# One attention and feed-forward layer on one Trainium2 core: softmax reciprocals spread over the partitions by DMA, heads normalised two pairs at a time, one more pair of heads in split products

## The chip, the cores and the metric

The kernel runs on one core of a Trainium2 chip. The metric is the device time of one execution in microseconds (us). The engines are PE (TensorE, matrix products), DVE (VectorE), ACT (ScalarE), POOL (GpSimd) and SP (SyncE, which issues the DMAs).

## The reference

The input is x of shape (16, 256, 128): 16 batches of 256 tokens. What is computed, cut to what matters:

```python
h = layernorm(x) * (1 + ca) + sa
q = h @ Wq                        # 16 heads of 64
k, v = split(h @ Wkv)             # 4 heads of 64 each, every one shared by 4 heads of q
q, k = rotary(q), rotary(k)
attn = softmax(q @ k.T * 64 ** -0.5)
x = x + ga * ((attn @ v) @ Wo + bo)
h = layernorm(x) * (1 + cb) + sb
x = x + gb * (gelu(h @ bin(w1).T + b1) @ bin(w2).T + b2)
```

`sa, ca, ga, sb, cb, gb` come from a small product with the input c, one row for each batch; `bin` keeps the signs of a weight and one scale for each output.

## The kernel before, in words

Every engine has a program written out by hand, and semaphores are the only order between engines. The attention runs over the 16 batches in steps (`attention_steps`); a step has 8 slots, and a slot works on one pair of heads. The table `SLOTS` is the order of the work inside a step: each string is a slot, each word a piece of work, and every engine walks through the same words and does its own part of each. The pieces overlap three batches: a step does the attention of its own batch, prepares q, k and v of the next one, and finishes the batch before.

The words: `S0` and `S1` are the two score products of a pair (PE), followed by the exponentials (ACT). `m` is a product with v of the pair before (PE, `product_with_v`): a pair in `SPLIT_PAIRS` is computed in six fp32r products of split operands, for which ACT computes the exponential twice (`probs`, `probs_hi`) and POOL subtracts (`probs_lo`); the other pairs take two plain fp32 products. `s0` to `s15` find the row maxima of a head (PE product, DVE reduction), `mT0` to `mT3` transpose them four heads at a time. `qkv..`, `kt`, `qt` make q and k; `yT` is the product with Wo, `zT` brings it back to the residual.

At the start of a slot ACT copies the unnormalised output of an older pair, with its row of softmax sums, from PSUM to `o_un` (word `un`, line 668). The eight pairs of a batch form half 0 (pairs 0 to 3) and half 1 (pairs 4 to 7). For each half SP gathers the sums into `sums` over 128 partitions (`gather_sums`, line 438), DVE takes the reciprocals and splits them in two fp32r parts (`recip0`, `recip1`, lines 790 to 794), SP writes those into `recip_parts` (`spread_reciprocals`, line 445), and for each pair a PE product with the constant `select` (words `bc0` to `bc7`, line 967) repeats them over 64 partitions for each head. DVE multiplies `o_un` by that, once for each head (line 777), into `o_t`, which `yT` reads.

SP has one queue and issues in program order, waiting on a semaphore ahead of each DMA. Besides the sums and reciprocals it moves, for each four heads of a batch, the high parts of q (`high_parts`, line 425: 64 partitions of 4 KB) and the transposed maxima (`maxima`, line 431, into partition 64 of `q_him`). The scores of slots 0, 2, 4 and 6 wait for both of these:

```python
if s % 2 == 0 and jc == 0:
    pe.wait_ge(q_him_in[s // 2], st.count(32, 32))
```

A last step (`tail`) finishes batch 15 beside the feed-forward part, which then runs over all batches.

Of the kernel before, what the change touches and what calls it, by code (L numbers as in the profile page):

```python
# [72 lines left out]
def parsed(slots):  # L73

    every, n, found = " ".join(slots).split(), 0, []
    for text in slots:
        slot, product = [("un",)], 0
        for word in text.split():
# [53 lines left out]
SPLIT_PAIRS = (1, 3, 4, 5, 7)  # L132
# [74 lines left out]
def slot_parts(st, s):  # L207

    if st.tail and s > 1:
        parts = [("part", u, part, part == PARTS[u[0]] - 1) for _, u in units(st, s) for part in range(PARTS[u[0]])]  # L210
        return [("recip", 1)] * (s == TAIL_RECIPROCALS_AT) + parts
    held = {"scores": st.attn, "pv": st.attn if s >= 1 else st.out, "un": st.attn if s >= 2 else st.out,
            "stats": st.norm, "rstd": st.norm, "norm": st.norm}
    return [w for w in ORDER[s]
            if (not st.tail and has(st, w[1]) if w[0] == "part" else not st.tail and (st.attn, st.out)[w[1]] if w[0] == "recip"
# [52 lines left out]
def adaln_layer(nc, x, wq, wkv, wo, bo, w1, b1, w2, b2, c, wmod, cos, sin, out):  # L268
    ctx = ExitStack()
    with ctx:  # L270
# [51 lines left out]
        q_him = [sb(f"q_him{i}", [DH + 1, 4, N], F32R) for i in range(2)]  # L322
# [4 lines left out]
        o_un = sb("o_un", [DH + 1, PAIRS, 2, N])  # L327
# [3 lines left out]
        recip_hi = sb("recip_hi", [P, 16], F32R)  # L331
        recip_lo = sb("recip_lo", [P, 16], F32R)
# [70 lines left out]
        def _(sp):  # L403
# [44 lines left out]
            def step(st):  # L448
# [6 lines left out]
                if st.out:  # L455
                    spread_reciprocals(st, 1, -1)
# [671 lines left out]
```

## Time and profile before

| | |
|---|---|
| median of 3 runs | 700.21 us (699.74 to 702.76) |
| the profiled execution | 700.25 us, span from first to last instruction 698.5 us |
| PE busy | 668.9 us (96%) |
| ACT, DVE, POOL busy | 551.4, 516.5, 430.1 us |
| mean granted TensorE clock | 0.99 |

How to read it: the span is what the trace covers, and the time of the execution is 1.75 us more. A busy share tells how long an engine had something under way, not that it ran at its peak. In the steady part one step, that is one batch, takes 37.7 us (the product with Wo comes back at that spacing).

### The profile page before, as it was taken

The numbers are of one execution on the slowest core, as the hardware profiler recorded it, in microseconds if no ns is written. First come the engines' busy times: TensorE is split into PE (matmuls) and PEld (weight loads), VectorE is DVE, ScalarE is ACT, GpSimd is POOL, SyncE is SP. The second block draws the span as 40 slices with busy tenths as digits, with TensorE's granted clock in tenths as the row PEclk, the third lists the DMA queues.
The fourth block names the chain that finished last, engine by engine and source line by source line (L and its number), as shares of the span: only waits on it lengthen the run. The fifth ranks groups of instructions, "written<-read, shape, count | busy, mean of one in ns | idle before, by whom it ended". The sixth has DMA issues, their size and how long they took to land.

```text
span 698.5 us, 13530 instructions
## 1 busy us (share of the span) xinstructions
PE 668.9 (96%) x3733; PEld 519.5 (74%) x3733; DVE 516.5 (74%) x1196; ACT 551.4 (79%) x1149; POOL 430.1 (62%) x397
## 2 busy tenths in 40 slices
PE   4698999999999999999999999999999999998897
PEld 3566787877777787878787777778787878667786
DVE  6566777778788777777787778887777877778762
ACT  4478887888787888878887878787887888768676
POOL 1657685857686776768585768577676758543110
PEclk9699999999999999999999999999999999999999
DMA  8111111011111111111102111111111110200111
GB/s 241 31 32 33 33 26 39 18 38 28 32 31 32 32 20 29 32 32 32 31 16 43 20 32 31 32 32 28 26 27 33 32 34 18 48 17 3 39 39 46
DMA packets 31580, 24.75 MB, mean 35 GB/s; under 512 B 16688, under 2 KB 26944, under 8 KB 31552
## 3 DMA queue, kind: packets, MB, share of 16 engines
q1 hardware_dynamic: 31552, 24.40, 16.6%
q8 instruction: 14, 0.23, 0.2%
q14 instruction: 14, 0.11, 0.1%
HBM read 4.47 MB, written 2.10 MB: 9 GB/s over the span
## 4 chain that ended last, share of the span: by engine, by line
PE 90%; DVE 3%; ACT 3%; POOL 1%; issue 1%; DMA 0%; SPq 0%; POOLq 0%; DVEq 0%
PE o_ps L1021 15%; PE o_ps L1011 11%; PE unit_ps L957 9%; PE score_ps L992 8%; PE unit_ps L946 8%; PE score_ps L994 8%; PE unit_ps L973 8%; PE o_ps L1078 4%; PE unit_ps L931 3%; PE unit_ps L932 3%; PE unit_ps L933 3%; PE unit_ps L967 2%; PE unit_ps L961 2%; PE unit_ps L1055 1%; PE unit_ps L1056 1%
## 5 line engine op out<-in xcount | busy, mean ns | idle before, releaser
L521 POOL TENSOR_TENSOR probs_lo<-probs,probs_hi 128x512 fp32r<-128x512 f32 x160 | 202.1, 1283 | 67.7 <-ACT probs_hi L662 67.6
L772 DVE TENSOR_REDUCE w_all<-unit_ps 128x2 f32<-128x512 f32 x256 | 166.2, 685 | 52.4 <-PE unit_ps L957 50.9
L659 ACT ACTIVATE probs<-score_ps 128x512 f32<-128x512 f32 x256 | 150.6, 589 | 21.2 <-PE score_ps L994 18.6
L507 POOL TENSOR_TENSOR rot_sum<-rot_a,rot_b 128x512 f32<-128x512 f32 (+1 forms) x96 | 104.7, 1097 | 99.3 <-DVE rot_b L764 99.0
L511 POOL TENSOR_TENSOR qk_rot<-rot_sum,qk_rot 128x512 fp32r<-128x512 f32 (+1 forms) x96 | 105.0, 1101 | 36.3 <-ACT qk_rot L609 36.3
L957 PEld LDWEIGHTS unit_ps<-k_hi,q_hilo 128*128 128x128 f32 x512 | 88.7, 191 | 41.3 <-issue 17.9
L957 PE MATMUL unit_ps<-k_hi,q_hilo 128*128 128x256 f32 x512 | 118.3, 318 | 0.7 <-ACT q_hilo L591 0.4
L946 PEld LDWEIGHTS unit_ps<-ident_r,qk_rot 128*128 128x128 f32 x640 | 101.9, 194 | 17.7 <-issue 4.3
L946 PE MATMUL unit_ps<-ident_r,qk_rot 128*128 128x128 f32 x640 | 110.2, 264 | 4.6 <-POOL qk_rot L511 3.8
L992 PE MATMUL score_ps<-q_hilo,k_hi 128*128 128x512 f32 x256 | 112.9, 441 | 1.1 <-DMA q_him<-neg_max_t 1.1
L777 DVE TENSOR_TENSOR o_t<-o_un,unit_ps 64x256 f32<-64x256 f32 x248 | 103.5, 417 | 4.4
L994 PE MATMUL score_ps<-q_him,k_lo 65*128 65x512 f32 x256 | 101.4, 396 | 0.0
L1011 PE MATMUL o_ps<-probs,v_whole 128*65 128x512 f32 x192 | 98.0, 592 | 0.0
L662 ACT ACTIVATE probs_hi<-score_ps 128x512 fp32r<-128x512 f32 x160 | 94.1, 588 | 0.0
L591 ACT ACTIVATE q_hilo<-unit_ps 128x512 fp32r<-128x512 f32 x128 | 76.4, 597 | 9.2 <-PE unit_ps L946 9.0
L668 ACT ACTIVATE o_un<-o_ps 65x512 f32<-65x512 f32 x128 | 74.4, 581 | 1.4 <-PE o_ps L1021 0.6
L762 DVE TENSOR_TENSOR rot_a<-unit_ps,cos_sb 128x512 f32<-128x512 f32 (+1 forms) x96 | 57.2, 596 | 21.6 <-PE unit_ps L961 17.1
L992 PEld LDWEIGHTS score_ps<-q_hilo,k_hi 128*128 128x128 f32 x256 | 48.5, 189 | 16.3 <-issue 8.9
L1021 PE MATMUL o_ps<-probs_hi,v_hi 128*65 128x512 f32 x160 | 60.3, 395 | 0.0
L1021 PE MATMUL o_ps<-probs_hi,v_lo 128*65 128x512 f32 x160 | 59.9, 411 | 0.0
L973 PE MATMUL unit_ps<-o_t,wo_sb 128*128 128x128 f32 x480 | 59.5, 277 | 0.0
L609 ACT ACTIVATE qk_rot<-rot_sum 128x512 fp32r<-128x512 f32 (+1 forms) x96 | 52.3, 561 | 6.7 <-POOL rot_sum L507 6.7
(120 smaller groups left out, 1123.4 us busy)
## 6 DMA issues: line engine op xcount, KB each, us to landing
q_him<-q_hilo SPq DMA_DIRECT2D x64, 256.0 KB
out_x<-w_all SPq DMA_DIRECT2D x16, 128.0 KB, 1.8
xa<-in_L_attn_x SPq DMA_DIRECT2D x3, 640.0 KB, 7.5
q_him<-neg_max_t SPq DMA_DIRECT2D x64, 4.0 KB
w_all<-in_L_attn_Wq SPq DMA_DIRECT2D x1, 512.0 KB, 5.3
w_sb<-in_L_ffn_w SPq DMA_DIRECT2D x2, 256.0 KB, 3.0
wo_sb<-in_L_attn_Wo SPq DMA_DIRECT2D x1, 512.0 KB, 8.2
sums<-o_un SPq DMA_DIRECT2D x32, 8.0 KB, 2.0
```

The costliest lines, as they stand in the source:

```text
L507: pool.tensor_tensor(total, rot_a[k % 2][:, 0:heads, :], rot_b[k % 2][:, 0:heads, :], ALU.add).then_inc(rot_summed, 1)
L511: pool.tensor_tensor(low, total, high.bitcast(F32), ALU.subtract).then_inc(rot_ready, 1)
L521: pool.tensor_tensor(probs_lo[s % 2][:, jc, :, :], probs[s % 2][:, jc, :, :], probs_hi[s % 2][:, jc, :, :].bitcast(F32), ALU.subtract).the ...
L659: ins = act.activation(probs[s % 2][:, jc, :, :].rearrange("p h i -> p (h i)"), score_ps[jc][:, :], ACT.Exp, scale=SCALE)
L772: dve.tensor_reduce(neg_max[u[1] // 4][:, first:first + C], ps[:, :].rearrange("p (c j) -> p c j", c=C), AX.X, ALU.max, negate=True).then_ ...
L946: ins = pe.matmul(ps[:, part * P:(part + 1) * P], qk_rot[:, ch, first + h, :, :].rearrange("p t d -> p (t d)"), ident_r[:, :], start=True, ...
L957: ins = pe.matmul(ps[:, ch * N:(ch + 1) * N], q_hilo[par][:, h, ch * P:(ch + 1) * P], k_hi2[par][:, g, :], start=True, stop=True)
L973: ins = pe.matmul(ps[:, own], wo_sb[:, s, :], o_t[:, s, own], start=s == 0, stop=s == PAIRS - 1)
L992: pe.matmul(ps[:, :], k_hi2[par][:, g, js], q_hilo[par][:, hs, :].rearrange("p h i -> p (h i)"), start=True, stop=False)
L994: pe.matmul(ps[:, :], k_lo1[par][:, g, js], q_him[s // 2 % 2][:, s % 2 * 2:s % 2 * 2 + 2, :].rearrange("p h i -> p (h i)"), start=False, s ...
L1011: ins = pe.matmul(o_ps[i][0:DH + 1, :], v_whole[par][:, jc, g, :], probs[i][:, jc, :, :].rearrange("p h i -> p (h i)"), start=jc == 0, sto ...
L1021: ins = pe.matmul(o_ps[i][0:DH + 1, :], v[par][:, jc, g, :], p[i][:, jc, :, :].rearrange("p h i -> p (h i)"), start=part == 0, stop=part == 5)
```

## The change

The reciprocals no longer pass through PE. After DVE has taken the 128x16 reciprocals of a half, one DMA writes them as one row of 2,048 values in a single partition (`reciprocals_to_row`, partition 96 for half 0 and 97 for half 1, in spare rows of the `q_him` buffer). When that has landed, two DMAs (`reciprocals_to_all`) copy the row's two parts of 1,024 values (4 KB) to 64 partitions each, into `o_t`. Another DMA (`second_heads`) moves the second heads of a half from partitions 0 to 63 of `o_un` to partitions 64 to 127. DVE then multiplies two pairs with both heads in one operation of 128x512 (`normalise_heads`, words `mul0` to `mul3`) in place. The `bc` words, `select`, `recip_parts` and the split of the reciprocals are gone. Pair 2 joins `SPLIT_PAIRS`. The table of slots is dealt anew: `mul0` and `mul1` stand in slot 0 of the next step, `mul2` and `mul3` at the end of slot 3. ACT's copy into `o_un` now waits for the multiplication that read the place before.

```diff
...
-    "S0 s9 m recip1 s10 qt6 qt6 qt6 qt6 m S1 s11 m m m m qkv00 mT2",
-    "qkv10 S0 m s12 m m S1 bc4 bc5 qt7 qt7 qt7 qt7 m bc6 m m s13",
-    "S0 bc7 S1 m s14 m s15 kt0 m kt0 stats kt0 rstd kt0 kt1 norm m m kt1 kt1 kt1 m mT3 yT0",
...
+    "S0 m recip1 s9 s10 m m S1 s11 qt6 m qt6 qkv00 qt6 m qt6 mT2 m",
+    "S0 s12 m m S1 qkv10 kt0 m m qt7 qt7 qt7 qt7 kt0 mul2 m kt0 s13 kt0 m mul3",
+    "S0 m s14 m s15 S1 kt1 m stats kt1 m rstd kt1 m kt1 m yT0 mT3",
...
+    "S0 qkv01 yT1 m m norm S1 qt0 m qt0 m qt0 qt0 m qt1 qt1 recip0 qt1 qt1 m qt2 qt2 zT0 zT0 qt2 qt2",
+    "S0 s0 m s1 s2 m m m s3 S1 m m qkv11 mT0",
...
+TAIL_PRODUCTS_AT = 6
+TAIL_AT = {("yT", 0): 7, ("yT", 1): 8, ("zT", 0): 9}
...
-SPLIT_PAIRS = (1, 3, 4, 5, 7)
+SPLIT_PAIRS = (1, 2, 3, 4, 5, 7)
...
-        q_him = [sb(f"q_him{i}", [DH + 1, 4, N], F32R) for i in range(2)]
+        q_him_all = sb("q_him_all", [P, 8, N], F32R)
+        q_him = [q_him_all[:, 4 * i:4 * i + 4, :] for i in range(2)]
+        recip_rows = [q_him_all[96 + i:97 + i, :, :].bitcast(F32) for i in range(2)]
         neg_max_t = [sb(f"neg_max_t{i}", [4 * C, P], F32R) for i in range(2)]
         probs = [sb(f"probs{i}", [P, C, 2, N]) for i in range(2)]
         probs_hi = [sb(f"probs_hi{i}", [P, C, 2, N], F32R) for i in range(2)]
         probs_lo = [sb(f"probs_lo{i}", [P, C, 2, N], F32R) for i in range(2)]
-        o_un = sb("o_un", [DH + 1, PAIRS, 2, N])
+        o_un = sb("o_un", [P, 2, 2, 4, N])
...
-        recip_hi = sb("recip_hi", [P, 16], F32R)
-        recip_lo = sb("recip_lo", [P, 16], F32R)
-        recip_parts = [sb(f"recip_parts{i}", [P, N], F32R) for i in range(2)]
-        select = sb("select", [P, PAIRS, DH], F32R)
...
-                    sp.dma_start(recip_parts[half][first:first + PAIRS, :].bitcast(F32).rearrange("h (b t) -> h b t", t=16),
-                                 part[:, :].bitcast(F32)).then_inc(recip_in[half], 16)
+                sp.dma_start(sums[:, :], o_un[DH:DH + 1, half, :, :, :]
+                             .rearrange("o h s (b t) -> o (h s b) t", t=16)).then_inc(sums_in[half], 16)
+
+            def second_heads(st, half, batch):
+
+
+                sp.wait_ge(sums_in[half], st.count(16, 16, batch))
+                sp.dma_start(o_un[DH:P, half, 0, :, :].rearrange("p s i -> p (s i)"),
+                             o_un[0:DH, half, 1, :, :].rearrange("p s i -> p (s i)")).then_inc(second_in[half], 16)
+
+            def reciprocals_to_row(st, half, batch):
+
+                sp.wait_ge(recip_ready, st.count(2, half + 1, batch))
+                sp.dma_start(recip_rows[half][:, :, :].rearrange("o h (b t) -> o (h b) t", t=16),
+                             recip[:, :]).then_inc(rows_in[half], 16)
+
+            def reciprocals_to_all(st, half, batch):
+
+
+                sp.wait_ge(rows_in[half], st.count(16, 16, batch))
+                if half == 0 and not st.prep:
+                    sp.wait_ge(z_ready, B - 1)
+                for h in range(2):
+                    sp.dma_start(o_t[h * DH:h * DH + DH, 4 * half:4 * half + 4, :].rearrange("p s i -> p (s i)"),
+                                 recip_rows[half][:, 4 * h:4 * h + 4, :].rearrange("o s i -> o (s i)").unsqueeze(1).broadcast_to([1, DH, 4 * N])).then_inc(recip_in[half], 16)
 
             def step(st):
                 if st.attn:
@@ -453,15 +469,21 @@
                 if st.attn:
                     high_parts(st, 2, 0)
                 if st.out:
-                    spread_reciprocals(st, 1, -1)
+                    second_heads(st, 1, -1)
+                    reciprocals_to_row(st, 1, -1)
+                    reciprocals_to_all(st, 1, -1)
                 if st.attn:
                     maxima(st, 2, 0)
                     high_parts(st, 3, 0)
                     maxima(st, 3, 0)
                     gather_sums(st, 0, 0)
-                    spread_reciprocals(st, 0, 0)
+                    second_heads(st, 0, 0)
+                    reciprocals_to_row(st, 0, 0)
                 if st.prep:
                     high_parts(st, 0, 1)
+                if st.attn:
+                    reciprocals_to_all(st, 0, 0)
+                if st.prep:
                     maxima(st, 0, 1)
...
+                            pair = (s - 2) % 8
+                            if st.number != 0 and pair < 4:
+                                act.wait_ge(o_t_ready, st.count(4, pair // 2 + 1, -1))
+                            act.activation(o_un[0:DH + 1, pair // 4, :, pair % 4, :],
+                                           o_ps[s % 2][0:DH + 1, :].rearrange("p (h i) -> p h i", h=2),
                                            ACT.Copy).then_inc(o_un_ready, 1)
...
-                if kind == "bc":
-
-                    for h in range(2):
-                        ins = dve.tensor_tensor(o_t[h * DH:h * DH + DH, u[1], :], o_un[0:DH, u[1], h, :],
-                                                ps[h * DH:h * DH + DH, 0:N], ALU.mult)
-                    ins.then_inc(o_t_ready, 1)
...
                 dve.wait_ge(sums_in[half], st.count(16, 16, batch))
                 dve.reciprocal(recip[:, :], sums[:, :]).then_inc(recip_ready, 1)
-                dve.wait_ge(recip_ready, st.count(2, half + 1, batch))
-                dve.tensor_copy(recip_hi[:, :], recip[:, :]).then_inc(recip_hi_ready, 1)
-                dve.wait_ge(recip_hi_ready, st.count(2, half + 1, batch))
-                dve.tensor_tensor(recip_lo[:, :], recip[:, :], recip_hi[:, :].bitcast(F32),
-                                  ALU.subtract).then_inc(recip_lo_ready, 1)
+
+            def normalise_heads(st, quarter, batch):
+
+                half, two = quarter // 2, slice(2 * quarter, 2 * quarter + 2)
+                own = slice(quarter % 2 * 2, quarter % 2 * 2 + 2)
+                if quarter % 2 == 0:
+                    dve.wait_ge(second_in[half], st.count(16, 16, batch))
+                    dve.wait_ge(recip_in[half], st.count(32, 32, batch))
+                dve.tensor_tensor(o_t[:, two, :], o_un[:, half, 0, own, :], o_t[:, two, :], ALU.mult).then_inc(o_t_ready, 1)
...
-                    half = u[1] // 4
-                    if u[1] % 4 == 0:
-                        pe.wait_ge(recip_in[half], st.count(32, 32, ahead(u)))
-                    ins = pe.matmul(ps[:, 0:N], select[:, 2 * (u[1] % 4):2 * (u[1] % 4) + 2, :].rearrange("k h d -> k (h d)"),
-                                    recip_parts[half][:, :], start=True, stop=True)
...
```

SP's program in the first step of the loop, from the gathering of the sums of half 1 to the maxima of heads 8 to 11 (`q_him` is called `q_him_all` after the change). Before:

```order
L438 DMA sums<-o_un 128x1x16 [waits o_un_ready]
L424 REGISTER_ALU
L425 DMA q_him<-q_hilo 64x1024 [waits q_ready]
L443 ISA
L445 DMA recip_parts<-recip_hi 8x16x16 [waits recip_lo_ready]
L445 DMA recip_parts<-recip_lo 8x16x16
L430 REGISTER_ALU
L431 DMA q_him<-neg_max_t 1x8x128 [waits max_t_ready]
```

After the change, the same place:

```order
L438 DMA sums<-o_un 128x1x16 [waits o_un_ready]
L424 REGISTER_ALU
L425 DMA q_him_all<-q_hilo 64x1024 [waits q_ready]
L444 ISA
L445 DMA o_un<-o_un 64x1024 [waits sums_in1]
L450 ISA
L451 DMA q_him_all<-recip 1x128x16 [waits recip_ready]
L461 DMA o_t<-q_him_all 64x1x1024 [waits rows_in1]
L461 DMA o_t<-q_him_all 64x1x1024
L430 REGISTER_ALU
L431 DMA q_him_all<-neg_max_t 1x8x128 [waits max_t_ready]
```

Two small DMAs have become four: one of 64 partitions, the row, and two copies from one partition to 64 each. The DMA of the maxima stands behind all of them, and SP waits for the row to land before it goes on. For half 0 the same four stand ahead of the maxima of heads 0 to 3 of the next batch, with one difference: the high parts of those heads are issued between the row and the two copies.

DVE's program in slot 3 of the same step. Before, two of the four pairs of half 1, then the row maxima of head 13:

```order
L777 TENSOR_TENSOR o_t<-o_un,unit_ps0 64x256 [waits unit_full]
L777 TENSOR_TENSOR o_t<-o_un,unit_ps0 64x256
L744 REGISTER_ALU
L777 TENSOR_TENSOR o_t<-o_un,unit_ps2 64x256 [waits unit_full]
L777 TENSOR_TENSOR o_t<-o_un,unit_ps2 64x256
L744 REGISTER_ALU
L772 TENSOR_REDUCE w_all<-unit_ps3 128x2 [waits unit_full]
```

After the change, from the rotation of q ahead of it to the same maxima:

```order
L783 TENSOR_TENSOR rot_a1<-unit_ps2,cos_sb 128x512 [waits rot_summed]
L785 TENSOR_TENSOR rot_b1<-unit_ps2,sin_sb 128x512
L814 TENSOR_TENSOR o_t<-o_un,o_t 128x512 [waits recip_in1,second_in1]
L765 REGISTER_ALU
L793 TENSOR_REDUCE w_all<-unit_ps0 128x2 [waits unit_full]
L814 TENSOR_TENSOR o_t<-o_un,o_t 128x512
```

Behind the multiplication that waits for the copies (`recip_in1`) stand the row maxima of head 13 and all that follows on DVE.

## Rows read from the trace of the kernel before

**Rows 1.** The page: span, busy time of each engine, share of the DMA queue.

```profile
span 698.5 us, 13530 instructions
PE 668.9 (96%) x3733; PEld 519.5 (74%) x3733; DVE 516.5 (74%) x1196; ACT 551.4 (79%) x1149; POOL 430.1 (62%) x397
q1 hardware_dynamic: 31552, 24.40, 16.6%
```

**Rows 2.** The page: the chain that ended last.

```profile
PE 90%; DVE 3%; ACT 3%; POOL 1%; issue 1%; DMA 0%; SPq 0%; POOLq 0%; DVEq 0%
```

**Rows 3.** Windows: one step; two start windows. Busy by engine, granted clock, DMA share, GB/s.

```profile
core 0: us, PE busy (x) PEld busy (x) DVE busy (x) ACT busy (x) POOL busy (x), PEclk, DMA share, GB/s
137.80:175.50 37.70, 37.68 (x214) 29.04 (x213) 29.09 (x63) 30.91 (x65) 26.11 (x24) 1.00 0.16 30
20.00:30.00 10.00, 6.91 (x26) 5.89 (x27) 3.50 (x10) 7.14 (x13) 6.74 (x8) 0.50 0.00 0
30.00:40.00 10.00, 8.39 (x44) 6.30 (x44) 6.28 (x11) 5.40 (x13) 3.71 (x3) 0.84 0.27 54
```

**Rows 4.** Who waited for whom: PE's scores on the DMA of the maxima.

```profile
PE score_ps L992 <- DMA q_him<-neg_max_t: 1.1, 2, 0.7
PEld score_ps L992 <- DMA q_him<-neg_max_t: 1.0, 1, 1.0
```

**Rows 5.** Groups by line and form: count, busy us, mean ns, idle before.

```profile
L967 PE MATMUL unit_ps<-recip_parts,select 128*128 128x256 f32 x124 | 49.0, 436 | 0.0
L1011 PE MATMUL o_ps<-probs,v_whole 128*65 128x512 f32 x192 | 98.0, 592 | 0.0
L521 POOL TENSOR_TENSOR probs_lo<-probs,probs_hi 128x512 fp32r<-128x512 f32 x160 | 202.1, 1283 | 67.7 <-ACT probs_hi L662 67.6
L662 ACT ACTIVATE probs_hi<-score_ps 128x512 fp32r<-128x512 f32 x160 | 94.1, 588 | 0.0
L777 DVE TENSOR_TENSOR o_t<-o_un,unit_ps 64x256 f32<-64x256 f32 x248 | 103.5, 417 | 4.4
L794 DVE TENSOR_TENSOR recip_lo<-recip,recip_hi 128x16 fp32r<-128x16 f32 x32 | 22.2, 694 | 1.1
L792 DVE CAST recip_hi<-recip 128x16 fp32r<-128x16 f32 x32 | 10.3, 321 | 1.1
```

**Rows 6.** The chain in order of time: start us, us, piece.

```profile
309.62 0.93 PE o_ps L1021 x4
314.06 0.24 PE unit_ps L967 x2
314.69 0.86 PE o_ps L1011 x2
```

**Rows 7.** Windows around single DMAs (columns as in rows 3).

```profile
5.50:7.00 1.50, 0.00 (x0) 0.00 (x0) 1.43 (x5) 0.63 (x1) 0.71 (x1) 1.00 0.93 303
292.77:294.24 1.47, 1.47 (x10) 1.05 (x8) 1.00 (x3) 0.04 (x1) 0.92 (x1) 1.00 0.87 176
291.41:291.59 0.18, 0.18 (x3) 0.18 (x3) 0.04 (x1) 0.18 (x1) 0.00 (x0) 1.00 0.50 46
287.17:287.67 0.50, 0.50 (x7) 0.50 (x6) 0.30 (x1) 0.45 (x1) 0.12 (x1) 1.00 0.15 17
286.57:286.67 0.10, 0.10 (x3) 0.10 (x3) 0.10 (x1) 0.10 (x2) 0.00 (x0) 1.00 0.22 41
```

**Rows 8.** Timeline of SP: when those DMAs were issued.

```profile
285.26 0.67 SPq L431 DMA_DIRECT2D q_him<-neg_max_t  x1
285.98 0.55 SPq L438 DMA_DIRECT2D sums<-o_un  x1
290.13 0.65 SPq L445 DMA_DIRECT2D recip_parts<-recip_hi  x1
291.59 0.53 SPq L425 DMA_DIRECT2D q_him<-q_hilo  x1
```

**Rows 9.** Issue to landing of the sums' DMA, min/median/max.

```profile
DMA to landing us min/median/max: 2.0/2.0/2.1
```

**Rows 10.** Timeline: the two reciprocals of a step, and the scores four heads ahead.

```profile
288.04 0.25 DVE L790 RECIPROCAL recip<-sums 128x16 f32<-128x16 f32 x1 [0.57 <-DMA sums<-o_un]
297.81 0.40 PE L992 MATMUL score_ps<-q_hilo,k_hi 128*128 128x512 f32 x1
308.78 0.24 DVE L790 RECIPROCAL recip<-sums 128x16 f32<-128x16 f32 x1
315.74 0.40 PE L992 MATMUL score_ps<-q_hilo,k_hi 128*128 128x512 f32 x1
```

More of the change, by code:

```diff
@@ L210, in slot_parts @@
         parts = [("part", u, part, part == PARTS[u[0]] - 1) for _, u in units(st, s) for part in range(PARTS[u[0]])]
-        return [("recip", 1)] * (s == TAIL_RECIPROCALS_AT) + parts
+        return ([("recip", 1)] * (s == TAIL_RECIPROCALS_AT)
+                + [("mul", 2), ("mul", 3)] * (s == TAIL_PRODUCTS_AT) + parts)
     held = {"scores": st.attn, "pv": st.attn if s >= 1 else st.out, "un": st.attn if s >= 2 else st.out,
-            "stats": st.norm, "rstd": st.norm, "norm": st.norm}
+            "stats": st.norm, "rstd": st.norm, "norm": st.norm, "recip": (st.attn, st.out), "mul": (st.out,) * 4}
     return [w for w in ORDER[s]
-            if (not st.tail and has(st, w[1]) if w[0] == "part" else not st.tail and (st.attn, st.out)[w[1]] if w[0] == "recip"
+            if (not st.tail and has(st, w[1]) if w[0] == "part" else held[w[0]][w[1]] and not (st.tail and s > 1 - w[1] // 2) if w[0] in ("recip", "mul")
                 else held[w[0]])]
@@ L437, in gather_sums @@
                 sp.wait_ge(o_un_ready, st.count(8, 4 * half + 4, batch))
-                sp.dma_start(sums[:, :], o_un[DH:DH + 1, 4 * half:4 * half + 4, :, :]
-                             .rearrange("o s h (b t) -> o (s h b) t", t=16)).then_inc(sums_in[half], 16)
-            def spread_reciprocals(st, half, batch):
-                sp.wait_ge(recip_lo_ready, st.count(2, half + 1, batch))
-                for first, part in ((0, recip_hi), (32, recip_lo)):
-                    sp.dma_start(recip_parts[half][first:first + PAIRS, :].bitcast(F32).rearrange("h (b t) -> h b t", t=16),
-                                 part[:, :].bitcast(F32)).then_inc(recip_in[half], 16)
+                sp.dma_start(sums[:, :], o_un[DH:DH + 1, half, :, :, :]
[15 more added lines that the diff above has]
+                                 recip_rows[half][:, 4 * h:4 * h + 4, :].rearrange("o s i -> o (s i)").unsqueeze(1).broadcast_to([1, DH, 4 * N])).then_inc(recip_in[half], 16)
             def step(st):
@@ L553, in _ @@
             act.activation(ident_r[:, :], ident[:, :], ACT.Copy).then_inc(ident_r_ready, 1)
-            for half in range(2):
-                act.activation(select[32 * half:32 * half + 32, :, :],
-                               ident[0:32, 0:PAIRS].unsqueeze(2).broadcast_to([32, PAIRS, DH]), ACT.Copy).then_inc(select_ready, 1)
             act.wait_ge(wkv_in, 16)
@@ L901, in wait_for_reader @@
                     pe.wait_ge(max_t_ready, st.count(4, u[1] + 1, of))
-                if kind == "bc":
-                    pe.wait_ge(o_t_ready, st.count(8, u[1] + 1, of))
                 if kind == "yT":
@@ L1044, in mlp_step @@
                     pe.wait_ge(max_t_ready, 4 * B)
-                    pe.wait_ge(o_t_ready, 8 * B - 4)
                     pe.wait_ge(x2_ready, B - 1)
```

34 lines of the change are left out of this document (15 added, 19 removed), and 8 rows, old and new, of the table SLOTS.

## The prediction, made before the changed kernel ran

> **What bounds the kernel now.** I read the page first. PE is busy for 96% of the span, the next engine, ACT, for 79% [rows 1], and 90% of the chain that ended last is PE's own work, with DMA at 0% [rows 2]. The window of one step in the steady part says the same: 37.68 us of PE work in 37.70 us, beside 29.0 on DVE, 30.9 on ACT and 26.1 on POOL [rows 3]. So PE sets the time, at the rate of one instruction behind another, and every other engine has 7 to 12 us to spare in a step. The DMA engines are 16% busy. The one place where a DMA could reach PE is the wait of the scores for the maxima: it cost 1.1 us in two places, and 1.0 in a third, in the whole run [rows 4]. That wait is covered now with little to spare, and it is what I look at in the change.
>
> The profiled execution took 700.25 us, its span 698.5; the median of the runs is 700.21, so the sum below can start from 700.2.
>
> **What the change takes off PE.** The chain gives start-to-start costs, which the mean durations (436 and 592 ns, overlapped [rows 5]) don't. Two `bc` products cost 0.24 us [rows 6], and there are 128 (124 of them in the group in [rows 5]): 128 x 0.12 = 15.4 us. Pair 2 was two plain products of 0.86 us each (the trace has two records for each), and becomes six split ones, four of which cost 0.93 us [rows 6]: 1.72 - 1.40 = 0.32 us, 16 times, 5.1 us. Together PE loses 20.5 us of work, 1.3 us a step.
>
> **What it adds elsewhere, and why that is hidden.** ACT gets two more exponentials a step (2 x 0.59 us [rows 5]): 30.9 + 1.2 = 32.1 us. POOL gets two more subtractions of 1.28 us: 26.1 + 2.6 = 28.7 us. Both stay under the 36.4 us that PE would then need. DVE loses 16 multiplications of 0.417 us and the split of the reciprocals, and gets four of 128x512. These are not in the trace; the nearest group is 0.417 us for half the columns, so 0.4 to 0.9 us each, 3.6 us at most for the 7 taken off. One thing may make them longer: `recip_lo`, on 16 columns with both operands in SBUF, takes 694 ns in the mean where the cast beside it takes 321 [rows 5], so something holds such operations up by up to a microsecond. Four of them a step are covered by DVE's 8.7 us. If no transfer were late, the result would be 700.2 - 20.5 = 680 us.
>
> **The new transfers.** Before, nothing in a step reads more than 8 KB from one partition. Now two DMAs for each half read 4 KB from one partition 64 times over, 262 KB each. The trace has no such DMA, so I bound it by windows laid around five that it has. With 128 partitions and 4 KB pieces (the load of Wq) the rate is 303 GB/s; the high parts of q, 64 partitions to 64, 4 KB pieces, 262 KB in 1.47 us, go at 176 GB/s with the DMA engines 87% busy; the reciprocals, 64-byte pieces from 128 partitions, go at 46 GB/s with the engines 50% busy; the sums, 64-byte pieces again but out of a single partition, at 17 GB/s with the engines 15% busy [rows 7], issued at the times in [rows 8]. So for pieces of one size the rate falls to a third when they all come from one partition, and the engines stand idle meanwhile: it is the partition that is waited for. The other row with one partition on one side, the maxima written into partition 64 in pieces of 512 bytes, shows 41 GB/s [rows 7].
>
> That bounds a copy: 262 KB at 41 GB/s is 6.4 us, at 17 GB/s 15.4 us. Below them lies the case in which reading from one partition costs nothing extra, 1.5 us as for the high parts. I take 26 GB/s, between 17 (right direction, small pieces) and 41 (longer pieces, other direction): D = 10.1 us a copy, 20.2 us for the two of a half, while PE would have a step done in 36.4. The Trainium skill says why it should be so: in "SBUF — State Buffer", section "Door 1: The DMA port swizzle", DMA reaches SBUF through 16 ports of 27.2 GB/s, and partitions 0 to 3 share one. The halving from 128 to 64 partitions agrees with it (303 and 176 GB/s); for reads from a single partition no row here settles it. By its figure a copy takes 9.6 us, and the time below would be about 30 us less.
>
> **How that reaches PE.** SP's order puts the DMA of the maxima right behind the two copies (the order in the section on the change). They are on one queue, so its small pieces go when the copies' have gone, and the next scores that need them wait. From the reciprocals of a half to that point:
>
> - the reciprocals, 0.25 us [rows 10];
> - the second heads, issued just ahead of the row, as long as the high parts: 1.5 us [rows 7];
> - the row, issue to landing as for the sums: 2.0 us [rows 9];
> - the copies, issue to landing 2.0 us and 2D = 20.2 us of pieces;
> - semaphores and the maxima's own pieces: 0.1 us.
>
> That is 5.9 + 2D = 26.1 us. Against it stands PE's work up to the scores that wait. For half 1 the reciprocals come at 308.78 and the scores of slot 4 at 315.74: 7.0 us [rows 10]. In the new slots `kt0` moves in (4 x 0.1 us), three `bc` go, pair 2 is 0.3 us shorter, and `recip1` stands one reduction (0.6 us) earlier: 7.5 us. For half 0 it is 288.04 to 297.81, 9.8 us [rows 10], and about that after. So PE stands for 26.1 - 7.5 = 18.6 us in slot 4 and 26.1 - 9.8 = 16.3 us in slot 0 of the next step: 34.9 us a step. DVE's own wait in `mul2` stands behind the same copies and ends at the same time, so it adds nothing of its own; what ACT waits for (`o_t_ready` ahead of `o_un`) comes later in the step.
>
> Then the clock. At the start, after PE had waited, the granted clock was 0.50 from 20 to 30 us and 0.84 in the mean from 30 to 40 [rows 3], the lower of its two levels, for somewhere near 13 us. PE will stand twice a step for over 16 us, and I expect it to come back at the lower level and to lose something after each: between 0 and half of that stretch, 6.5 us. I take 1.5, so 3 us a step.
>
> **Sum.** A step gains 34.9 + 3.0 = 37.9 us and loses 1.3. Sixteen batches have both halves (those of the last end in the tail, where `mul2` waits beside the feed-forward part; I count them like the others): 700.2 + 16 x 37.9 - 20.5 = 1286. In the tail some of the wait has other work, so I say 1280 us. A step would take 74 us.
>
> Each microsecond of D is worth 64 us of time. With D = 6.4 the sum is about 1045, with 15.4 about 1620.
>
> **The rivals.**
>
> *The copies are as fast as the high parts* (D = 1.5 us). For it: their pieces are as long, and they write 64 partitions in the same way; if only the writing side limits a DMA, this holds. Against it: the 17 GB/s with engines 15% busy. The chain is then 8.9 us, against 7.5 and 9.8 us of cover: 1.4 us of wait a step, 16 x 1.4 = 22 us, which eats the 20.5 won: 700 us, no change. Under D = 0.8 us, or with the second heads not in the way, slot 4 doesn't wait and the time is 680 to 690, faster. That is the case on the other side; it turns at D = 1.5. Chances: 0.10 faster, 0.05 no change.
>
> *A partition can be read at about twice my rate*, 45 to 50 GB/s, because the 176 GB/s of the high parts were read and written on the same 64 partitions, that is 352 GB/s in and out together. Then D is about 5.5 us, the chain 16.9, the waits 9.4 and 7.1, the clock loses less: 700.2 + 16 x (16.5 + 1.5) - 20.5 = 968. Chance 0.14.
>
> *It is as slow as the 64-byte row*: D = 15.4, 1620 us. Chance 0.05.
>
> *An engine other than PE becomes the bound*: ACT would need 36.4 us of work a step and has 32.1. Near 685 us; a chance so small that it is counted with the fast copies.
>
> The main case has 0.66, with its own range of 1170 to 1400 (D from 9 to 11.5, clock 0 to 5 us a step).
>
> **Numbers.** I predict 1280 us. Left out below the range are the fast copies (0.15); left out above, the slowest (0.05). That gives 950 to 1420. A change under 0.5% can't be told from none here. Slower by over 0.5%: 0.66 + 0.14 + 0.05 = 0.85; within 0.5%: 0.05; faster: 0.10.
>
> **What would show it.** In the new trace: steps of about 74 us; two long waits of PE in a step, ahead of the scores of slots 0 and 4, put down to the DMA of the maxima; DVE idle ahead of the first multiplication of each half; windows inside those waits with 26 GB/s, no more, and PE's granted clock at its lower level after them; PE's busy share near 50%. No `bc`, six products for pair 2. If I am wrong, it is in D: a window on the copies then shows well over 26 GB/s, and at 176 the step is 36 to 38 us. If the copies are slow but the maxima's pieces pass them, the waits go to the multiplications, and the step is a little shorter.

## The result, and the profile after

The changed kernel takes 1247.66 us (median of 4 runs, 1246.77 to 1250.99) against 701.39 us for the kernel before beside it: a ratio of 1.780, 95% interval 1.774 to 1.786. The profiled execution has a span of 1244.9 us. Runs of one kernel mostly agree within 1%; where they spread further (e2, e5, e6) the range stands beside the median, and e1, e3, e4 and e8 were run once each.

The page of the changed kernel: span, busy time by engine, the DMA queue's share, the chain that ended last by engine, and (second part) issues with KB each and median us to landing:

```profile
span 1244.9 us, 13182 instructions
PE 706.6 (57%) x3637; PEld 556.2 (45%) x3637; DVE 432.3 (35%) x937; ACT 569.4 (46%) x1179; POOL 468.5 (38%) x429
q1 hardware_dynamic: 35136, 49.31, 55.7%
issue 42%; PE 26%; DMA 13%; POOL 13%; ACT 4%; DVE 2%; SPq 0%; POOLq 0%; ACTq 0%; DVEq 0%
...
o_t<-q_him_all SPq DMA_DIRECT2D x64, 256.0 KB, 16.3
o_un<-o_un SPq DMA_DIRECT2D x32, 256.0 KB, 3.4
```

Against [rows 1, 2]: PE's share went from 96% to 57%, and the chain that was 90% PE is now 42% "issue", time in which an engine waits for nothing that the profile can name. The pieces of the high parts of q, 256 KB (262,144 bytes, the 262 KB of the prediction), took 1.47 us [rows 7]; a copy of the same size out of one partition lands 16.3 us after its issue in the median (11.7 to 20.6, since the second copy of a half waits for the first).

Windows of the changed kernel (columns as in [rows 3]): one step; five rounds of pieces inside the copies; the stretch behind a wait; and the one after that.

```profile
567.00:638.60 71.60, 39.79 (x208) 31.20 (x207) 23.64 (x47) 32.13 (x67) 28.46 (x26) 0.79 0.58 37
612.14:624.19 12.05, 0.00 (x0) 0.00 (x0) 0.00 (x0) 1.51 (x3) 2.99 (x3) 0.65 0.95 27
628.30:632.70 4.40, 4.40 (x14) 3.63 (x15) 3.86 (x11) 1.72 (x4) 1.27 (x1) 0.50 0.00 0
632.70:638.60 5.90, 5.90 (x45) 5.43 (x45) 1.90 (x5) 4.33 (x9) 3.60 (x4) 1.00 0.02 2
```

A step takes 71.6 us. In this window inside the copies PE and DVE do nothing at all, all DMA engines are under way (0.95), and only 27 GB/s move. After the wait PE is busy the whole time, but does 14 products in 4.4 us where the next window has 45 in 5.9: the granted clock is 0.50, the lower level.

The timeline of one half (start us, duration us, engine, line; in brackets the idle time before it):

```profile
602.72 0.24 DVE L805 RECIPROCAL recip<-sums 128x16 f32<-128x16 f32 x1
603.08 0.60 SPq L445 DMA_DIRECT2D o_un<-o_un  x1
603.89 0.51 SPq L451 DMA_DIRECT2D q_him_all<-recip  x1
607.21 1.16 SPq L461 DMA_DIRECT2D o_t<-q_him_all  x2
608.49 6.35 SPq L431 DMA_DIRECT2D q_him_all<-neg_max_t  x1
614.95 9.49 SPq L425 DMA_DIRECT2D q_him_all<-q_hilo  x1
628.16 0.69 DVE L814 TENSOR_TENSOR o_t<-o_un,o_t 128x512 f32<-128x512 f32 x1 [18.05 <-DMA o_t<-q_him_all]
628.27 0.77 PE L1004 MATMUL score_ps<-q_hilo,k_hi 128*128 128x512 f32 x1 [17.02 <-issue]
...
663.57 0.79 PE L1004 MATMUL score_ps<-q_hilo,k_hi 128*128 128x512 f32 x1 [14.66 <-DMA q_him_all<-neg_max_t]
```

From the reciprocals of half 1 to the scores of slot 4 there are 25.6 us, and PE stands for 17.0 of them; for half 0 PE stands 14.7 us in slot 0 of the next step. The multiplication and the scores start within 0.11 us of each other, since both hang on the same queue. One thing the prediction didn't name: SP itself is stuck behind the copies. Issuing the maxima took it 6.35 us and the next high parts 9.49, where they took 0.67 and 0.53 in the kernel before [rows 8].

Who waited for whom (us in total, times, longest):

```profile
PE score_ps L1004 <- issue: 300.8, 18, 19.2
DVE o_t L814 <- DMA o_t<-q_him_all: 292.6, 16, 20.9
PE score_ps L1004 <- DMA q_him_all<-neg_max_t: 176.6, 13, 16.4
```

The two rows for L1004 are 31 waits and 477 us together, against 1.1 us before [rows 4]. For 18 of them the profile names no releaser ("issue"), for 13 it names the maxima; experiments 1 and 6 change both kinds alike, so it is the same cause. Over the whole trace PE's idle time went from 29.6 to 538.3 us (the span less the busy time on each page), which is 509 us more.

### The profile page after: what moved, and what is told of

The parts are those of the page before. It is cut to its first block, busy times and chain, and to the rows that moved or that the text cites. A ratio compares the mean times of both kernels' runs of the same rounds, so it can differ in the third digit from the quotient of the medians.

```text
span 1244.9 us, 13182 instructions
## 1 busy us (share of the span) xinstructions
PE 706.6 (57%) x3637; PEld 556.2 (45%) x3637; DVE 432.3 (35%) x937; ACT 569.4 (46%) x1179; POOL 468.5 (38%) x429
## 4 chain that ended last, share of the span: by engine, by line
issue 42%; PE 26%; DMA 13%; POOL 13%; ACT 4%; DVE 2%; SPq 0%; POOLq 0%; ACTq 0%; DVEq 0%
DMA q_him_all<-neg_max_t 9%; POOL probs_lo L543 8%; PE o_ps L1033 5%; PE score_ps L1004 3%; PE unit_ps L976 3%; PE score_ps L1006 3%; PE unit_ps L985 2%; POOL qk_rot L533 2%; POOL rot_sum L529 2%; PE o_ps L1089 2%; DMA o_t<-q_him_all 2%; DMA out_x<-w_all 2%; PE unit_ps L965 2%; PE o_ps L1023 1%; ACT k_hi L605 1%
## 5 line engine op out<-in xcount | busy, mean ns | idle before, releaser
L1004 PE MATMUL score_ps<-q_hilo,k_hi 128*128 128x512 f32 x256 | 123.4, 482 | 477.8 <-issue 300.8
L543 POOL TENSOR_TENSOR probs_lo<-probs,probs_hi 128x512 fp32r<-128x512 f32 x192 | 242.4, 1284 | 282.4 <-ACT probs_hi L681 282.3
L1004 PEld LDWEIGHTS score_ps<-q_hilo,k_hi 128*128 128x128 f32 x256 | 54.1, 211 | 494.0 <-issue 397.5
L814 DVE TENSOR_TENSOR o_t<-o_un,o_t 128x512 f32<-128x512 f32 x64 | 42.5, 686 | 292.6 <-DMA o_t<-q_him_all 292.6
L965 PE MATMUL unit_ps<-ident_r,qk_rot 128*128 128x128 f32 x640 | 134.6, 277 | 11.3 <-POOL qk_rot L533 9.3
L965 PEld LDWEIGHTS unit_ps<-ident_r,qk_rot 128*128 128x128 f32 x640 | 116.2, 203 | 44.1 <-issue 29.7
L976 PEld LDWEIGHTS unit_ps<-k_hi,q_hilo 128*128 128x128 f32 x512 | 107.3, 234 | 36.2 <-issue 15.9
L681 ACT ACTIVATE probs_hi<-score_ps 128x512 fp32r<-128x512 f32 x192 | 113.2, 590 | 0.0
L1006 PE MATMUL score_ps<-q_him_all,k_lo 65*128 65x512 f32 x256 | 112.5, 439 | 0.0
L1033 PE MATMUL o_ps<-probs_hi,v_hi 128*65 128x512 f32 x192 | 85.8, 476 | 0.0
L1033 PE MATMUL o_ps<-probs_lo,v_hi 128*65 128x512 f32 x192 | 69.7, 405 | 0.4 <-POOL probs_lo L543 0.4
L1023 PE MATMUL o_ps<-probs,v_whole 128*65 128x512 f32 x128 | 65.5, 594 | 0.1
## 6 DMA issues: line engine op xcount, KB each, us to landing
o_t<-q_him_all SPq DMA_DIRECT2D x64, 256.0 KB, 16.3
```

Of the source, the lines that this page charges most:

```text
L543: pool.tensor_tensor(probs_lo[s % 2][:, jc, :, :], probs[s % 2][:, jc, :, :], probs_hi[s % 2][:, jc, :, :].bitcast(F32), ALU.subtract).the ...
L681: ins = act.activation(probs_hi[s % 2][:, jc, :, :].rearrange("p h i -> p (h i)"), score_ps[jc][:, :], ACT.Exp, scale=SCALE)
L965: ins = pe.matmul(ps[:, part * P:(part + 1) * P], qk_rot[:, ch, first + h, :, :].rearrange("p t d -> p (t d)"), ident_r[:, :], start=True, ...
L976: ins = pe.matmul(ps[:, ch * N:(ch + 1) * N], q_hilo[par][:, h, ch * P:(ch + 1) * P], k_hi2[par][:, g, :], start=True, stop=True)
L1004: pe.matmul(ps[:, :], k_hi2[par][:, g, js], q_hilo[par][:, hs, :].rearrange("p h i -> p (h i)"), start=True, stop=False)
L1006: pe.matmul(ps[:, :], k_lo1[par][:, g, js], q_him[s // 2 % 2][0:DH + 1, s % 2 * 2:s % 2 * 2 + 2, :].rearrange("p h i -> p (h i)"), start=F ...
```

## The experiments

**Theory.** What costs the time is the number of bytes that leave one partition: 262 KB a copy, at 27.2 GB/s, with the maxima queued behind. Rivals: the time goes with the number of DMAs and semaphores, not with bytes; each partition is slow by itself, so that spreading the source over any four of them cures it; or only the order on SP's queue matters.

**1. Half the bytes, and none.** The copies move 2 KB instead of 4 KB to each partition (e1), or 64 bytes (e2). The multiplications become a maximum of the same size that reads `o_un` twice and not the reciprocals (that edit isn't shown), so the attention's output isn't normalised in both.

```diff
-  sp.dma_start(o_t[h * DH:h * DH + DH, 4 * half:4 * half + 4, :]..., recip_rows[half][:, 4 * h:4 * h + 4, :]...broadcast_to([1, DH, 4 * N]))
+  sp.dma_start(o_t[h * DH:h * DH + DH, 4 * half:4 * half + 2, :]..., recip_rows[half][:, 4 * h:4 * h + 2, :]...broadcast_to([1, DH, 2 * N]))  # e1
+  sp.dma_start(o_t[h * DH:h * DH + DH, 4 * half, 0:16], recip_rows[half][:, 4 * h, 0:16].unsqueeze(1).broadcast_to([1, DH, 16]))            # e2
```

> The two copies of each half move only the first two of their four pairs: 2 KB pieces instead of 4 KB, 131 KB a copy instead of 262. The multiplications read o_un twice and not o_t, so the output is not normalised; their waits, sizes and places are the changed kernel's. My theory: a copy is paced by the reads of one partition at 27 GB/s, so its time D falls from 9.6 to 4.8 us, each of the 32 waits of PE (14.5 and 17.0 us) gets 9.6 us shorter, and the time is 1248 - 32 x 9.6 = 940 us, or 10 to 30 less if the clock loses less after shorter waits. Rival, the copies cost mostly a fixed time (64 pieces from one place, whatever their length): the time stays within 100 us of 1248.

> The two copies of each half move 64 bytes to each of their 64 partitions (4 KB in all); the multiplications read o_un twice, so the output is not normalised. Everything else, the six DMAs of a half, the new slots and the sixth split pair, is the changed kernel's. My theory: the chain from the reciprocals to the maxima is then about 6 us, under the 7.5 and 9.8 us of PE's work that cover it, PE does not wait, and the time is 680 to 690 us. Rival, the number of transfers or the new slots cost something by themselves: over 700 us.

Measured: e1 945.94 us, PE's waits 7.3 and 4.9 us in turn instead of 17.0 and 14.5; e2 684.14 us (median of three runs, 681.3 to 689.6; a fourth took 2537.6 us for a reason that isn't known, and is left out), ratio 0.978, interval 0.971 to 0.985, with most steps at 36.6 to 36.8 us and no wait of PE over 2.5 us in the whole trace. The same DMAs, semaphores and order stand in all three. Half the bytes took 9.7 and 9.6 us off the two waits: the two copies of a half carry 262 KB less, which makes 27 GB/s. The bytes are the cause, and the change without them is faster than the kernel before.

**2. Four source partitions, side by side or apart.** SP writes the row into four partitions, and each DMA reads from all four, 16 copies from each: partitions 96 to 99 (half 0) and 100 to 103 (half 1) in e3, partitions 96, 100, 104 and 108 (half 1 one higher) in e4.

```diff
+                for p in range(96 + 4 * half, 100 + 4 * half):            # e3
+                for p in range(96 + half, 112 + half, 4):                 # e4
+                    sp.dma_start(q_him_all[p:p + 1, :, :]..., recip[:, :]).then_inc(rows_in[half], 16)
-                sp.wait_ge(rows_in[half], st.count(16, 16, batch))
+                sp.wait_ge(rows_in[half], st.count(64, 64, batch))
-                                 recip_rows[half][:, 4 * h:4 * h + 4, :]...broadcast_to([1, DH, 4 * N]))
+                                 q_him_all[96 + 4 * half:100 + 4 * half, 4 * h:4 * h + 4, :]...broadcast_to([4, 16, 4 * N]))   # e3
+                                 q_him_all[96 + half:109 + half:4, 4 * h:4 * h + 4, :]...broadcast_to([4, 16, 4 * N]))        # e4
```

> The row of reciprocals is written four times, into four neighbouring partitions (96 to 99 for half 0, 100 to 103 for half 1), and each copy reads 16 of its 64 pieces from each. Three more small DMAs lengthen the chain by about 1.9 us. My theory, with the Trainium skill (SBUF - State Buffer, Door 1): the four partitions are behind one port, so a copy still takes 9.6 us and the time is 1248 + 32 x 1.9 = 1310 us. Rival, each partition is limited by itself: a copy takes a quarter, 2.4 us, and the time is about 1248 - 32 x (14.4 - 1.9) = 850 us. With the next run it tells partition from port.

> As the run with four rows in neighbouring partitions, with the same number and size of DMAs, but the four rows lie 4 partitions apart (96, 100, 104, 108 and 97, 101, 105, 109). My theory: these are four ports, a copy takes about 2.5 us, and the time is near 1248 - 32 x (14.3 - 1.9) = 850 us, less some 30 us because the clock falls less. Rival, each partition is limited by itself: the same as the run with neighbouring partitions. Rival, neither helps because the limit is on the number of engines that take part: both near 1300 us.

Measured: e3 1354.18 us, PE's waits 20.5 and 17.4 us, 3 us longer than with one row, where I expected 1.9 for the three more DMAs. e4 898.62 us, waits 6.7 and 3.3 us. A window inside the copies of e3, where no other DMA runs, and one in e4, columns as above:

```profile
512.60:522.20 9.60, 0.00 (x0) 0.00 (x0) 0.00 (x0) 0.00 (x0) 0.00 (x0) 0.50 0.24 25
```

```profile
521.80:527.30 5.50, 3.96 (x18) 2.37 (x16) 1.98 (x3) 4.77 (x11) 4.70 (x4) 1.00 0.26 89
```

Both have a quarter of the DMA engines under way, and move 25 and 89 GB/s: four neighbours are read no faster than one partition (27), four partitions that lie four apart more than three times as fast. What is scarce is shared by neighbours, and it is not the DMA engines. The Trainium skill says so in "SBUF — State Buffer", "Door 1: The DMA port swizzle": partitions 0 to 3 lie behind one port of 27.2 GB/s, 4 to 7 behind another. The runs agree for the partitions they use (96 to 99 together, 96, 100, 104 and 108 apart), and with the figure as a limit. Whether the 89 GB/s of e4 are set by its four source partitions or by the quarter of the DMA engines that takes part isn't tested. e4 is still slower than before the change, and some 50 to 80 us above my expectation: its two copies of a half take about 3 us each (262 KB at 83 to 89 GB/s) and not 2.5, and three more DMAs for the rows stand ahead of them.

**3. The row in HBM.** The row is written to a small tensor in HBM and the copies read it from there; nothing else changes (e5). In e6 SP also issues the row ahead of the second heads of half 1.

```diff
-                sp.dma_start(recip_rows[half][:, :, :]..., recip[:, :]).then_inc(rows_in[half], 16)
+                sp.dma_start(rows_dram[half].rearrange("(p t) -> p t", t=16), recip[:, :]).then_inc(rows_in[half], 16)
-                                 recip_rows[half][:, 4 * h:4 * h + 4, :]...broadcast_to([1, DH, 4 * N]))
+                                 rows_dram[half, 4 * N * h:4 * N * (h + 1)].unsqueeze(0).broadcast_to([DH, 4 * N]))
...
-                    second_heads(st, 1, -1)       # e6 alone
                     reciprocals_to_row(st, 1, -1)
+                    second_heads(st, 1, -1)       # e6 alone
```

> The row of reciprocals of a half is written to a small tensor in HBM instead of one partition, and both copies read it there; sizes, places and number of the DMAs are the changed kernel's. My theory, the copies are slow only because one partition is read: they now go like the high parts of q, 1.5 us each, the chain from the reciprocals to the maxima is 5.9 + 3.0 = 8.9 us against 7.5 and 9.8 us of PE's work, PE waits 1.4 us a step, and the time is 690 to 705 us. Rival, sixty-four reads of the same 4 KB are slow wherever they lie: over 1000 us.

> As the run with the row in HBM, and for half 1 SP issues the row ahead of the second heads, so that it doesn't queue behind their 1.5 us. The chain is then 7.4 us, within PE's 7.5: no wait, 677 to 688 us, and faster than before. If the run with the row through HBM is as fast, the second heads were not in the way.

Measured: e5 768.97 us (three runs at 768.0 to 770.6 and one at 737.5; the trace is of the slowest), well off what I expected. The copies are as fast as I thought: a window on the two of one half, and their median to landing:

```profile
427.90:430.50 2.60, 2.08 (x15) 1.58 (x14) 1.29 (x2) 1.36 (x4) 2.60 (x4) 1.00 0.77 192
...
o_t<-rows_dram SPq DMA_DIRECT2D x64, 256.0 KB, 4.0
```

192 GB/s instead of 27, though 64 partitions read one row. But 8 of its 15 steps take 45 to 46 us, not 36.6, and there PE waits up to 6.7 us for DVE. The waits and the timeline of e5, same step:

```profile
PE unit_ps L964 <- DVE w_all L792: 58.6, 13, 6.7
...
431.36 7.68 DVE L813 TENSOR_TENSOR o_t<-o_un,o_t 128x512 f32<-128x512 f32 x1 [1.71 <-DMA o_t<-rows_dram]
432.30 1.31 POOL L532 TENSOR_TENSOR qk_rot<-rot_sum,qk_rot 128x512 fp32r<-128x512 f32 x1
433.55 1.29 POOL L528 TENSOR_TENSOR rot_sum<-rot_a,rot_b 128x512 f32<-128x512 f32 x1
434.77 2.50 POOL L542 TENSOR_TENSOR probs_lo<-probs,probs_hi 128x512 fp32r<-128x512 f32 x2
437.21 1.28 POOL L532 TENSOR_TENSOR qk_rot<-rot_sum,qk_rot 128x512 fp32r<-128x512 f32 x1
438.97 0.68 DVE L792 TENSOR_REDUCE w_all<-unit_ps 128x2 f32<-128x512 f32 x1
439.70 0.48 PE L964 MATMUL unit_ps<-ident_r,qk_rot 128*128 128x128 f32 x1 [6.36 <-DVE w_all L792]
```

The multiplication that takes 0.69 us in the changed kernel takes 7.68 here. It begins while POOL works and ends only after POOL's last operation in a row of them (437.21 + 1.28 = 438.49), and PE waits behind DVE. In the changed kernel POOL had next to nothing to do when the late copies landed, and none of the 64 multiplications took over 0.69 us, so the slow copies hid this. e6: 692.05 us (682.5 to 695.9), ratio 0.985, interval 0.980 to 0.989. In its trace, of the fastest run, the longest multiplication takes 1.79 us, and steps are 36.6 to 36.9 us.

**4. The same, with one input in SBUF.** e5 with the four multiplications of a step replaced by an operation of the same size that reads only `o_un`; it leaves the normalisation out.

```diff
-                dve.tensor_tensor(o_t[:, two, :], o_un[:, half, 0, own, :], o_t[:, two, :], ALU.mult).then_inc(o_t_ready, 1)
+                dve.tensor_reduce(o_t[:, two, :], o_un[:, half, 0, own, :].unsqueeze(3), AX.X, ALU.max).then_inc(o_t_ready, 1)
```

> As the kernel with the row in HBM (e5: 769 us), with its order of DMAs, but the four multiplications of a step are replaced by an operation of the same 128x512 on DVE with a single input in SBUF: a maximum over an axis of length one, which copies o_un to o_t. So the normalisation is left out; every wait, DMA and slot stays. Theory: e5's multiplications of up to 7.9 us are held up because both of their inputs are in SBUF, where POOL reads too, while POOL runs one operation behind another. Then all 64 take 0.6 to 0.8 us, PE never waits 6 us ahead of L964, no step takes 45 us, and the time is 680 to 695 us. Rival: what holds them is the place (something that comes just after a transfer has landed in o_t, or a semaphore), whatever they read. Then about 14 of 64 still take over 1.3 us, some 7 us, and the time is 735 to 770 us.

Measured: 689.58 us (688.0 to 690.2), ratio 0.983, interval 0.982 to 0.985. The group in e9 and in e5 (busy us, mean ns, idle before):

```profile
L813 DVE TENSOR_REDUCE o_t<-o_un 128x512 f32<-128x512 f32 x64 | 42.0, 679 | 29.1 <-DMA o_t<-rows_dram 29.1
```

```profile
L813 DVE TENSOR_TENSOR o_t<-o_un,o_t 128x512 f32<-128x512 f32 x64 | 113.6, 1796 | 29.4 <-DMA o_t<-rows_dram 29.4
```

All 64 now take 673 to 689 ns, at the same places behind the same DMA, and the 45 us steps are gone. So it is neither the place nor the DMA. e9 changes the kind of operation along with its inputs; the trace of e5 tells these apart, for its rotations are of the same kind and size, with one input in PSUM (durations in ns, least, median and most):

```profile
L782 DVE TENSOR_TENSOR rot_a<-unit_ps,cos_sb x96: 410/691/693, 15.2 to 666.5; 128x512 f32<-128x512 f32 x64, 128x256 f32<-128x256 f32 x32
L784 DVE TENSOR_TENSOR rot_b<-unit_ps,sin_sb x96: 410/679/681, 15.5 to 667.1; 128x512 f32<-128x512 f32 x64, 128x256 f32<-128x256 f32 x32
```

None of them was held up, though over half began while POOL worked. It is the second input in SBUF. The Trainium skill gives the rule in "SBUF — State Buffer", "Who interferes with whom": DVE's second SBUF read shares a port with POOL's, and whoever issues first has it for its instruction. The traces agree, with an addition: here DVE waited through the rest of one operation of POOL and five more in a row, 7.7 us, and not through one of 1.3.

**5. The sixth pair alone.** The kernel before, with only pair 2 added to `SPLIT_PAIRS` (e7); and the kernel e6 with pair 2 taken out again (e10).

```diff
-SPLIT_PAIRS = (1, 3, 4, 5, 7)           # before, to e7
+SPLIT_PAIRS = (1, 2, 3, 4, 5, 7)
-SPLIT_PAIRS = (1, 2, 3, 4, 5, 7)        # e6, to e10
+SPLIT_PAIRS = (1, 3, 4, 5, 7)
```

> The kernel before with pair 2 in SPLIT_PAIRS and nothing else. My sum gave this part 5.1 us off PE: 696 us. Rival, the slots of before leave no room in pair 2's place for two more exponentials on ACT and two subtractions on POOL (2.6 us), whose result the last two products wait for: no gain, or 2 to 6 us slower.

> The kernel with the row in HBM and issued ahead of the second heads (e6: 692 us median), with pair 2 back in plain fp32 products, so five split pairs as before the change. If the sixth pair costs in these slots what it cost alone in the old ones (e7: plus 8 us), the time is 681 to 686 us. If it is worth what the prediction's term says (two plain products of 0.86 us against six of 1.40 in sum), the time is 5 us above e6, 697 us. In the profile POOL then has 2.6 us less work a step, and DVE's multiplications are held up less often.

Measured: e7 708.60 us (707.3 to 710.1), ratio 1.0126, interval 1.011 to 1.014: 8.8 us slower by the ratio, where my term has 5.1 us less. e10 677.02 us (675.9 to 679.5), ratio 0.967, interval 0.965 to 0.969: the fastest of all, 24 us faster than before, with steps of 36.1 to 36.3 us. The sixth pair costs something in the new slots too, for all six runs of e6 are slower than all five of e10, but e6 spreads too far to say how much: 5.5 us between the two fastest traces (682.5 and 677.0), 12 by the two ratios, 15 between the medians. Where it goes in e7, waits and groups (compare L792 and L794 with [rows 5]):

```profile
PE unit_ps L961 <- DVE w_all L772: 9.1, 16, 1.1
...
L792 DVE CAST recip_hi<-recip 128x16 fp32r<-128x16 f32 x32 | 20.2, 630 | 1.1
L794 DVE TENSOR_TENSOR recip_lo<-recip,recip_hi 128x16 fp32r<-128x16 f32 x32 | 27.2, 849 | 1.1
L702 DVE TENSOR_SCALAR var_eps<-mean_var 128x2 f32<-128x2 f32 x32 | 24.4, 762 | 1.1
```

and the same wait, and the group of L702, in the kernel before:

```profile
PE unit_ps L961 <- DVE w_all L772: 1.2, 2, 1.0
...
L702 DVE TENSOR_SCALAR var_eps<-mean_var 128x2 f32<-128x2 f32 x32 | 20.0, 626 | 1.1
```

Beside the two extra subtractions of a step on POOL, three small DVE operations that work within SBUF grow by 9.9, 5.0 and 4.4 us in sum, all but a microsecond of DVE's growth (516.5 to 536.5 us busy), and PE waits for DVE 16 times instead of 2. In the kernel before, 16 of the 32 `recip_lo` began while POOL worked and took 1.21 us in the mean, the other 16 took 0.18; in e7 it is 21 of 32. Between the two traces (spans of 698.5 and 705.5 us) PE's idle time grows by 8.6 us, of which the wait rows are 7.9, and its busy time falls by 1.6, not by 5.1. That POOL's extra work is what moves these operations fits the traces; e7 adds two exponentials a step on ACT as well, and they weren't tried apart.

**6. The maxima ahead of the copies.** The changed kernel with the two orders on SP turned round, so that the maxima which the next scores need are no longer queued behind the copies (e8).

```diff
-                    reciprocals_to_all(st, 1, -1)
+                    if not st.attn:
+                        reciprocals_to_all(st, 1, -1)
                 if st.attn:
                     maxima(st, 2, 0)
+                    if st.out:
+                        reciprocals_to_all(st, 1, -1)
...
+                if st.prep:
+                    maxima(st, 0, 1)
                 if st.attn:
                     reciprocals_to_all(st, 0, 0)
                 if st.prep:
-                    maxima(st, 0, 1)
```

> The changed kernel with SP's order turned: the DMAs of the maxima that stood behind the two copies are issued ahead of them. My theory: DVE's first multiplication of a half waits for the same copies, and PE needs DVE's reductions soon after, so the wait only moves from the scores to a unit product and the time stays within 60 us of 1248. Rival, PE is held by the maxima in the queue alone: its waits go and the time is under 900 us.

Measured: 1238.03 us. The waits of e8:

```profile
DVE o_t L818 <- DMA o_t<-q_him_all: 520.3, 31, 20.4
PE unit_ps L969 <- DVE w_all L797: 241.6, 14, 17.3
PE unit_ps L980 <- DVE rot_b L789: 179.0, 14, 12.9
```

The scores hardly wait any more (13.5 us in two places, all in all), but DVE stands in the multiplications, and behind it are the reductions and rotations that PE needs: 17.3 and 12.9 us a step. The order decides where the copies are paid, not what they cost.

## Why the prediction was right, point by point

**Only the copies matter: right.** e2, without their bytes, is at 684 us; half of them give 946, all of them 1248. Two copies in 19.2 to 19.3 us (five rounds of pieces at 27 GB/s) make D = 9.6 us, where I took 10.1: 0.5 us by 64 takes 30 us from the sum of 1286; the other two misses below are 25 us down and 14 up. The 26 GB/s between 17 and 41 were a choice, and that it fell so near is in part luck. The 27.2 GB/s of the Trainium skill ("SBUF — State Buffer", "Door 1: The DMA port swizzle"), which the prediction set beside it, was the better number.

**The chain and the waits: right in place, a little long.** Predicted 26.1 us from reciprocals to scores, measured 25.6 (half 1) and, from 639.50 to 663.57, 24.1 (half 0). Predicted waits 18.6 and 16.3, measured 17.0 and about 14.5, 31.5 us a step instead of 34.9. Of these 3.4 us (54 us in the run) D is 1.8 (30 us); the other 25 us are cover (8.5 us instead of 7.5 ahead of slot 4) and, for half 0, the shorter way of the row. DVE's wait adds nothing of its own, as said (it ends 0.11 us from PE's), but e8 shows that it would have cost nearly as much by itself (1238 us). The prediction had the step "a little shorter" if the maxima got past the copies, and that is what e8 does.

**The clock: right in kind, too small.** I took 1.5 us lost for each wait. The granted clock stayed at its lower level for 4.3 us after the long wait and 3.4 after the short one, at half rate 2.1 and 1.7 us lost, 3.9 a step instead of 3.0: 14 us more in the run.

**The sum with what was measured:** 700.2 - 20.5 + 16 x (31.5 + 3.9) = 1246 us, the measured time within 2. The waits of one step stand in it 16 times; the totals of the trace bear them out, with 509 us more of PE's idle time (16 x 31.5 = 504) and a busy time 60 us above that of e6, which has the same products (706.6 against 646.5, where 16 x 3.9 = 62). What the waits and clock leave of a step is 71.6 - 31.5 - 3.9 = 36.2 us, and 36.4 was predicted.

**The 20.5 us that PE loses: nearly right in the sum, by luck, and wrong in its parts.** It hid two errors of opposite sign. Pair 2 was to save 5.1 us, and costs 7 to 9 us in the old slots and 5 to 15 in the new ones; PE's busy time with the pair split is 646.5 us (e6) and without it 646.2 (e10), so the saving itself doesn't show. I had costed its two subtractions on POOL at nothing, under POOL's free time. `recip_lo`'s 694 ns were in my rows as a sign that something holds DVE up, but I applied it to the new multiplications alone and not to DVE operations that were there already. The other way round, the path of the reciprocals without PE is worth more than 128 x 0.12 = 15.4 us: e10 is 24 us faster than before. Its trace has nearly the whole gain in PE's busy time (668.9 to 646.2 us), and PE's idle time as it was (29.6 and 29.0), so the other 8 us aren't in waits that the profile shows; where they come from stays open. For the changed kernel the two hardly matter, since both are small beside 566 us of waits and clock.

**"Up to a microsecond" for the multiplications: wrong as a bound.** With the copies slow they took 0.69 us. With the copies fast they took up to 7.9 us (e5). The rival "copies as fast as the high parts" was priced at 700 us; with copies that fast the runs give 738 to 771 us in the same order of DMAs, or 692 with the row first. Had the copies been fast, I would have been wrong for this reason.

**Small slips in the sums.** By the prediction's own terms D = 6.4 us gives 1049 us and not 1045, and 15.4 gives 1625 and not 1620; neither touches the forecast. PE's busy share, expected near 50%, is 57%.

**The rivals:** 17 GB/s and 45 to 50 GB/s are both excluded by the window at 27; no other engine became the bound.

## What to carry to other kernels

A DMA that repeats a row over partitions costs by where the row lies: out of one partition, or four neighbours, it went at 25 to 27 GB/s, out of four that lie apart at 89, out of HBM at 192; what stands behind it on the same queue waits as long. Before work is given to an engine with free time, look at what that engine's operations share with the one that feeds the critical engine: here POOL's free 11 us a step were not free for DVE. The version to use is the change with its row in HBM, issued first, and five split pairs: 677 us against 701.

## What the runs showed of the hardware that was not expected

- A DVE operation with both inputs in SBUF was held for 7.7 us while POOL ran five operations one behind another; the same size with one input in SBUF took 0.68 us at the same place. Small operations are held too: the 128x16 subtraction for `recip_lo` took 1.21 us in the mean where it began while POOL worked and 0.18 where it didn't, and a cast of 128x16 grew from 321 to 630 ns in the mean when POOL had 2.6 us more work a step.
- SP takes part in the waiting: the issue of one DMA behind the copies took 6.35 and 9.5 us, where it took 0.67 and 0.53 in the kernel before.
- After standing for 14 to 17 us PE ran for 3.4 to 4.3 us at the lower clock level. The loss doesn't shrink with the wait: in e4 4 to 6 us at that level followed waits of 6.7 us, and after most of those of 3.3 us the clock fell for 3.4 us, 1 to 2 us after PE had begun again; in e1 3 to 6 us followed waits of 7.3 and 4.9.
- Sixty-four partitions read the same 4 KB of HBM at 192 GB/s, no slower than the high parts of q between SBUF partitions (176 GB/s, [rows 7]).
